# Attention and experts on one core: value products issued ahead of the tasks of maxima

## What is computed

```
h = layernorm(x) * (1 + ca) + sa
q, k, v = split(h @ W_attn + b_attn)
att = softmax(q @ k.T / sqrt(8) + alibi + causal)
x = x + ga * (att @ v @ W_proj + b_proj)
h = layernorm(x) * (1 + cb) + sb
x = x + gb * sum_e(combine[:, e] * (silu(h @ w1[e].T) @ w2[e].T) * expert_scale[e])
```

## Time and profile before

| | |
|---|---|
| profiled execution, its time | 674.69 us |
| its span, first to last instruction | 672.9 us |
| mean granted TensorE clock | 0.951 |
| TensorE matmuls busy | 591.6 us, 88% |
| VectorE busy | 540.7 us, 80% |
| ScalarE busy | 478.5 us, 71% |
| GpSimd busy | 88.0 us, 13% |
| T, line 583 | 118.6 us busy, 640 matmuls |
| S, line 643 | 115.0 us busy, 640 matmuls |
| V, line 611 | 178.9 us busy, 2432 matmuls |
| exponentials, line 1104 | 298.9 us busy, 576 of 571 ns mean |
| reductions of tasks, line 871 | 328.2 us busy, 320 of 1061 ns mean |

### The profile page before, as it was taken

One profiled execution on the slowest core, in us unless ns is written; L12 is line 12 of the kernel. 1 busy time (PEld: TensorE's weight loads), 2 busy tenths in 40 slices (PEclk: granted clock), 3 DMA queues, 4 the chain that ended last, 5 costly groups with the idle time before them and its releaser, 6 DMA issues. The chain is left out here.

```text
span 672.9 us, 14690 instructions
## 1 busy us (share of the span) xinstructions
PE 591.6 (88%) x5838; PEld 320.5 (48%) x5838; DVE 540.7 (80%) x840; ACT 478.5 (71%) x925; POOL 88.0 (13%) x166
## 2 busy tenths in 40 slices
PE   4657778899899999799999988996899999999996
PEld 3313232432433333234324233553687778787784
DVE  3798999899798889798998899555667888777775
ACT  4812557688688888788897788666558678675872
POOL 3320000100000100620000805341000000000000
PEclk9955899999898999999999899999799999999998
DMA  5781500000600006600000000000422200342100
GB/s 151 232 242 31 75 2 2 3 3 3 100 5 2 2 4 250 105 1 2 4 2 3 2 2 2 2 1 1 111 50 47 63 0 1 99 100 49 36 0 16
DMA packets 34200, 30.40 MB, mean 45 GB/s; under 512 B 2956, under 2 KB 32332, under 8 KB 33868
## 3 DMA queue, kind: packets, MB, share of 16 engines
q1 hardware_dynamic: 33800, 29.09, 17.3%
q10 hardware_dynamic: 336, 0.42, 0.2%
HBM read 21.90 MB, written 7.41 MB: 44 GB/s over the span
## 5 line engine op out<-in xcount | busy, mean ns | idle before, releaser
L1104 ACT ACTIVATE probs<-b 128x512 f32<-128x512 f32 (+1 forms) x576 | 298.9, 571 | 91.3 <-PE b L643 39.7
L871 DVE TENSOR_REDUCE part<-b 128x2 f32<-128x1024 f32 (+2 forms) x320 | 328.2, 1061 | 39.6 <-PE b L583 18.6
L611 PE MATMUL pv<-probs,v_cur 128*32 128x256 f32 (+1 forms) x2432 | 178.9, 378 | 1.0 <-ACT probs L1104 0.9
L643 PE MATMUL b<-aug 55*128 55x512 bf16 (+3 forms) x640 | 115.0, 358 | 36.3 <-ACT probs L1104 33.8
L583 PE MATMUL b<-aug 52*128 52x512 bf16 (+3 forms) x640 | 118.6, 369 | 18.5 <-DVE part L871 15.8
L1131 ACT ACTIVATE probs<-b 128x512 f32<-128x512 f32 x128 | 81.3, 635 | 46.7 <-PE b L741 46.4
L993 DVE TENSOR_TENSOR hs_lo<-probs,hs_hi 128x512 fp32r<-128x512 f32 x128 | 86.6, 695 | 29.5 <-ACT hs_hi L1131 28.8
L643 PEld LDWEIGHTS b<-aug 55*128 55x128 bf16 x640 | 36.7, 93 | 146.2 <-ACT probs L1104 136.3
L611 PEld LDWEIGHTS pv<-probs,v_cur 128*32 128x32 f32 x2432 | 51.7, 110 | 77.8 <-issue 48.6
L1131 ACT ACTIVATE hs_hi<-b 128x512 fp32r<-128x512 f32 x128 | 82.4, 644 | 0.0
L739 PE MATMUL b<-h_hi,w_hi 128*128 128x512 f32 (+1 forms) x128 | 52.4, 410 | 0.7 <-DVE hs_lo L993 0.5
(11 more groups left out here) (136 smaller groups left out, 498.9 us busy)
## 6 DMA issues: line engine op xcount, KB each, us to landing
yn<-comb_scratch SPq DMA_DIRECT2D x32, 256.0 KB, 5.2
aug<-q_scratch SPq DMA_DIRECT2D x6, 384.0 KB
aug<-k_scratch SPq DMA_DIRECT2D x6, 384.0 KB
w1T_sb<-in_w1T SPq DMA_DIRECT2D x1, 2048.0 KB, 7.6
w2T_sb<-in_w2T SPq DMA_DIRECT2D x1, 2048.0 KB, 13.6
q_scratch<-pieces SPq DMA_DIRECT2D x4, 384.0 KB, 2.9
k_scratch<-pieces SPq DMA_DIRECT2D x4, 384.0 KB, 3.4
x_sb<-in_x SPq DMA_DIRECT2D x4, 256.0 KB, 6.2
```

Source lines behind the costliest of these rows:

```text
L611: return mm(pv[32 * hh:32 * hh + 32, c0:c1], v_cur[:, kb, hh, :], probs[:, step_ % 2, hh, at_:at_ + c1 - c0], start=(kb == 0 and c0 == 0), ...
L643: done.append(mm(pair[half][:, at_:at_ + w], k_aug[g % 2][n, b, kb * P:kb * P + P], q_aug[g % 2][n, b, (j + 1) * CW - w:(j + 1) * CW], sta ...
L871: ins = nc.vector.tensor_reduce(dst, b1[:, slot:slot + 2, at_:at_ + w], AX.X, ALU.max)
L1104: nc.scalar.activation(probs[:, p % 2, hh, 0:w], b2[:, (n2 - 1) % RING2, 0:w], ACT.Exp).then_inc(exp_done, 1)
```

## The change

In each half step `pass1` is called behind the value products and no longer ahead of them. It still stands ahead of the projection in the last group, and the turn of maxima at the end of a step still stands behind everything. What is computed, the number of tasks in each half step and all other engines' programs stay as they are.

```diff
                             scores(p, b)
-                            pass1(min(PLAN[first][p][b], NTASK) if last else PLAN[first][p][b])
                             if p >= 1 and p - 1 not in START[first:NC_]:
                                 value_products(p, b)
                             elif p >= 1 and b == PAIRS - 1:
                                 for half in range(PAIRS):
                                     value_products(p, half)
+                            pass1(min(PLAN[first][p][b], NTASK) if last else PLAN[first][p][b])
                             if last and p in PROJECT:
```

## The result

The changed kernel took **677.15 us** (median of 20 runs, 674.10 to 680.13), the kernel before 674.06 (20 runs, 670.18 to 678.36). The ratio is 1.0044 with a 95% interval of 1.0024 to 1.0063: slower by 3 us, just inside the 0.5% that the prediction called no change. Forecast were 673.7 us, 668.0 to 681.5, and +0.8 us in the sum. So the range and the case held, and the size of the sum did not. The 3 us are clear of the interval, and most of this part is about where they lie. (Four executions in the whole study took far longer than their kernel's others, 697.87 and 1770.41 us for the new order in groups 1 to 3 alone, 1193.87 and 1050.44 us for the kernel before, and are left out of medians, ratios and fits.)

What follows compares the result with a forecast made beforehand. VectorE was taken to pace group 0, and the loop of scores, exponential and three score banks the other groups. Terms 0 + 1.1 + 0.1 + 1.0 - 0.9 - 0.5 = +0.8 us gave 673.7 us, range 668.0 to 681.5.

Steps and rivals of the forecast that it cites:

- the case: Whole kernel: time within 0.5% (3.4 us) of the kernel before, called no change; chance 0.50.
- The steady half steps: Half steps between masks: the new order fits the loop's 1.23 and 1.17 us, so 0 us.
- V waits as before: Rival, b = 0 half steps: value products start 0.19 us behind their exponential, not 0.05; +5.8 us, chance 0.22.
- Tasks with masks: Diagonals and last 128 queries: mask matmuls lengthen half steps, 0.09 us per diagonal, +1.1 us in all.
- The lower bound: Masked tasks: with 0.46 us from value products to task in place of 0.57, -1.2 us in all.
- Maxima and their turn: Turns of maxima: tasks come 0.74 us later, GpSimd's cut has 0.66 us to spare; +0.1 us for a few turns.
- My own sum for b = 0: Half steps b = 0 without masks: 0.39 + 0.57 + 0.22 = 1.18 us, below the loop's 1.23.
- (a): Group 0, step 1, b = 0: the task behind value products reaches VectorE later, +1.0 us.
- (b): Group 0, step 4, b = 1: value products run while the task's bank is read, ending VectorE's idle time; -0.9 us.
- (c): Group 0, end of the stretch paced by VectorE: turn and scores follow the last held task at once, -0.5 us.
- VectorE's idle time goes: Rival, group 0's paced stretch: better feeding removes most of 7.9 us idle; 666.7 us, or 670 with half; chance 0.16.
- The clock falls elsewhere: Rival: two more or two fewer half-clock stretches of TensorE, 677 or 670 us; chance 0.08 for more, 0.04 for fewer.

Runs made afterwards that it cites:

- the old order with the useless matmuls: Kernel before, with each task's matmuls issued three times in the half steps of groups 1 to 3 without value products: 666.94 us, ratio 0.9915.
- the one kernel that put two steps back: New order with tasks issued three times where TensorE waited, but old order in steps 1 and 7 of group 0: 672.50 us, ratio 0.9958.
- The last kernel: Old order with repeated tasks and matmuls at attention's end, plus group 0's tasks ahead of step 1 issued twice: 668.03 us, ratio 0.9899.

## Why the prediction was right, and where it was not

**The steady half steps: right.** The term was 0, and all its parts were found: 1.23 and 1.17 us, V 0.40 and 0.32 behind S, 0.06 behind the exponential (347.13 to 347.19), T 0.57 behind V. The tasks issued twice show that it holds even without the loop's room.

**"V waits as before": refuted.** 58 waits of 0.10 us would have been 5.8 us. V in its new place waits as in the earlier trace rows, with 0.06 for 0.05.

**Tasks with masks: too high.** +1.1 us was forecast, about 0.1 measured: b = 0 went from 1.235 to 1.246 us. The step that failed is "S to V 0.39": I took the steady distance into a half step that follows a longer one, where the exponential is early. The lower bound, 0.46 from V to T, did not come either. Here the Trainium skill ("TensorE: Matmul & The Clock Gate", section "Step-by-step: what each phase is for") speaks of weight loads that are pulled ahead of running matmuls. From V to T this case's traces show 0.57 to 0.58 us in every kernel, from V to the turn 0.46, so what the prediction worked out from that rule did not hold between V and T; the measurement decides. Between S and T, both row-tiled, the trace agrees: T's loads run 0.21 us ahead.

**Maxima and their turn: the step that failed most.** "+0.1 us for a few such turns" was worked out from GpSimd's slack at one turn (124.62 to 125.28) and took the changes between the two kinds of matmul as free. In groups 1 to 3 five half steps, (2, 1) and (20, 1), grew from 1.297 to 1.510 us, +1.1 us together, with no wait in them at all; the turn put between V and T took this back, which shows the cause. This step of the working failed: it priced a turn by GpSimd's slack alone. And the turn of step 7 in group 0 had no slack: it waited 0.65 us for the cut before and 1.21 now, and its half step grew by 0.68. I had read one turn and spoken for all.

**The short half steps: missing from the sum.** The five half steps (9, 0) and (20, 0) grew from 1.09 to 1.19 us, +0.5. My own sum for b = 0, 1.18, was right for them; I had compared it with a loop of 1.23 that holds for 512-wide scores alone. Putting the old order back in these and in the steps 35, which had grown by 0.03 to 0.10, gave 1.0 us back, give or take 0.4.

**Group 0: one sign wrong, two sizes wrong, the largest growth missing.** Forecast were +1.0 (a), -0.9 (b) and -0.5 (c). Measured: (a) the half step behind the first V grew by 0.49. (b) Half steps (4, 1) and (5, 0) did fall by 1.18 and 0.75 us, but the trace of before has a stretch at half clock there, from 78.1. Against the old order with the useless matmuls, which has none there, (4, 1) fell by 0.50 and (5, 1) rose by 0.44; from (4, 0) to (6, 0) the sum is -0.3, a third of the forecast. So a good part of the 0.87 us of idle time in the earlier trace rows was probably that stretch's, and not the order's. (c) Step (20, 1) grew by 0.21 and (19, 0) by 0.22 where -0.5 was forecast. The largest growth, the +0.68 of the turn in step 7, was in no term. The whole group comes to +1.6 us against that undisturbed trace (120.48 less 118.90), and the kernel with the new order in group 0 alone measured +1.9 us.

**"VectorE's idle time goes": refuted.** It was 7.9 us in the kernel before and 8.6 in the changed one; with the useless matmuls 6.8 and 9.7.

**"The clock falls elsewhere": half right.** The number of stretches does change, from run to run in each kernel, and at about 1.1 us for each (3.4 us at half clock are 0.0025 of the mean clock) they are most of the spread. They don't explain the difference, since the changed kernel's mean clock was no lower.

**The sum.** Groups 1 to 3: turns 1.1, short half steps 0.5, ends of groups and the steps behind them some 0.2 to 0.4, in all about 1.8 to 2.0, measured +2.0. Group 0: about 1.6, measured +1.9. Together 3.5 at equal clock. That the forecast of +0.8 still fell in the right case is owed to errors of both signs: masks forecast 1.0 too high, turns, short half steps and group 0 some 3.8 too low. The net error, 2.7 us, is over three times the forecast, and the ratio of 1.0044 stopped just short of 0.5%: that part of the hit is luck. What stays open is which wait of group 0 is the cause and which the consequence: they move from half step to half step, and the one kernel that put two steps back shows no clear gain. So of the 3.5 us the cause is shown for the turns and the short half steps of groups 1 to 3; for the ends of groups and for group 0 only the place is.

## What to carry to other kernels

When an order of matmuls is changed, count the changes between row-tiled and full matmuls in each half step, not only in the commonest one: here each was worth 0.1 us, and outside group 0 the loss sat in the half steps with a turn or with short exponentials, while the steady ones were untouched. A loop's room must be measured at the width at which it is used. And where a kernel's runs spread by more than the effect, bring the mean clock of each run into the comparison, or take the cause of the spread away first.

## What the runs showed of the hardware

- **Useless matmuls pay where the clock would fall.** 673.1 us (the kernel before, timed beside it), 666.9 with three times the tasks in the few half steps in which TensorE stood waiting, 664.8 (timed beside 674.6 for the kernel before) with 25 further matmuls around the end of attention. The spread fell from 7 to 1 us in the first of them. In groups 1 to 3 the half clock came behind gaps that were short. Ahead of the stretch of the earlier trace rows TensorE waited for an exponential for 0.86 us (ahead of 280.44) and then stood for 0.90 us more (ahead of 281.95), which is the stall of step (4, 1): the exponentials that this V reads had ended (with the useless matmuls it starts 0.55 us behind its S, at 276.86, and here 1.51 us behind it). Ahead of the stretch from 375.1 us stands the wait of 0.86 us alone. The same wait of 0.86 us stands in traces where no stretch follows, as at 278.29 in that of the kernel with the old order in the short half steps. The Trainium skill ("TensorE: Matmul & The Clock Gate", section "HAM oscillation — how this bites in real kernels") tells of long gaps of TensorE that bring the half clock back; this case's traces agree in kind, but show it also behind gaps as short as these.
- **In the long stretch ahead of attention they cost more than they gave.** The last kernel raised TensorE's busy time there from 22.7 to 31.1 us, and it took 3.3 us more, with a higher mean clock in most runs (0.974 on average against 0.971).
- **Weight loads run ahead within a kind of matmul, not across:** 0.21 us from S to T, 0.11 from V to the turn, 0.00 to 0.03 from S or T to V, from V to T and S, and from T to the turn or the turn to S.
- **Distances at full clock, the same in every trace:** S to T 0.21 to 0.22 us, S to V 0.29 to 0.32, T to V 0.31, T to turn 0.32, V to turn 0.46, V to T 0.57 to 0.58. Behind V a matmul of the same kind comes 0.11 us sooner than a row-tiled one.
- **4.4 us for each 0.01 of mean clock,** over 14 kernels, with 1.05 us of scatter. Within the 85 runs of the kernel before it is 5.2, and the granted clock alone gives 83% of the variance of their times.
